# A graph block with gated experts on one core: the expert pairs all in the attention stage, and a combination in five parts with TensorE summing most pairs

## The reference

```
x = x + segment_sum(LN(x)[src] * edge_weight, dst) @ W + b       # layer 1
y = LN(x)
h = y @ W_gat                                   # 4 heads x 4 experts
a = leaky_relu(a_src[src] + a_dst[dst])         # 131072 edges + one loop per node
agg = segment_softmax(a) weighted sum of h[src], by dst, + b_gat
scores = LN(agg) averaged over the heads        # 4 per node
g = softmax over the 2 best scores, 0 for the other experts
out = x + sum over e of g[e] * (gelu(y @ W1[e] + b1[e]) @ W2[e] + b2[e])
```

## Time and profile before

| | us |
|---|---|
| median of 3 runs | 6031.14 (6027.12 to 6062.34) |
| the profiled execution, its own time | 6026.56 |
| its span (first to last instruction) | 6024.8 |

### The profile page before, as it was taken

One profiled execution on the slowest core, in us unless ns is written; L12 is line 12 of the kernel. 1 busy time (PEld: TensorE's weight loads), 2 busy tenths in 40 slices (PEclk: granted clock), 3 DMA queues, 4 the chain that ended last, 5 costly groups with the idle time before them and its releaser, 6 DMA issues. The chain is left out here.

```text
span 6024.8 us, 57614 instructions
## 1 busy us (share of the span) xinstructions
PE 3403.8 (56%) x13477; PEld 2557.7 (42%) x13478; DVE 1931.2 (32%) x4962; ACT 756.9 (13%) x2073; POOL 2722.3 (45%) x2817
## 2 busy tenths in 40 slices
PE   1354445455556776777822227964475665749266
PEld 0233333343444454555511116853354453628145
DVE  5435454645453444333300001221111020202359
ACT  4100000000000111111200001211011111202122
POOL 4465544454545555555377771043615243340420
PEclk6576666676767887888855558976677776869578
DMA  7422222222222333333100001111111111101348
GB/s 224 132 87 74 80 66 73 61 82 68 77 64 83 92 93 91 93 96 97 60 25 11 13 9 35 47 43 24 34 32 37 29 41 25 46 19 54 121 147 323
DMA packets 289866, 437.42 MB, mean 73 GB/s; under 512 B 60488, under 2 KB 223539, under 8 KB 288563
## 3 DMA queue, kind: packets, MB, share of 16 engines
q0 software_dynamic: 114208, 216.64, 13.5%
q1 hardware_dynamic: 77503, 127.56, 5.9%
q10 hardware_dynamic: 98004, 91.50, 4.7%
HBM read 329.96 MB, written 105.97 MB: 72 GB/s over the span
## 5 line engine op out<-in xcount | busy, mean ns | idle before, releaser
L633 POOL DMA_INDIRECT rows<-feats,src_t x1500 | 1457.2, 971 | 1285.3 <-PE node_sums L792 711.8
L1307 POOL DMA_INDIRECT got<-row_dram,src_sorted x1024 | 997.8, 974 | 1251.4 <-DMA state_dram<-got 914.8
L792 PE MATMUL node_sums<-rows,hot 128*128 x3904 | 1171.7, 459 | 667.9 <-issue 507.7
L792 PEld LDWEIGHTS node_sums<-rows,hot 128*128 128x128 f32 x3904 | 862.6, 230 | 945.7 <-issue 806.9
L1388 PE MATMUL d_hidden<-d_yt,w 128*128 128x256 f32 x2752 | 725.3, 402 | 584.4 <-issue 583.4
L1399 PE MATMUL d_expert<-w,hid 128*128 128x256 f32 x2752 | 723.2, 402 | 482.5 <-issue 480.6
L1388 PEld LDWEIGHTS d_hidden<-d_yt,w 128*128 128x128 f32 x2752 | 550.6, 201 | 727.7 <-issue 662.4
L1450 DVE TENSOR_TENSOR yo<-d_expert,b2r 128x512 f32<-128x512 f32 x172 | 119.0, 692 | 2230.8 <-remote 1391.9
L1399 PEld LDWEIGHTS d_expert<-w,hid 128*128 128x128 f32 x2752 | 552.1, 201 | 626.7 <-issue 560.1
L851 DVE TENSOR_SCALAR hot<-iota,rel,ew_t 128x128 f32<-128x128 f32 x1952 | 565.8, 362 | 99.2 <-issue 34.8
L1334 ACT ACTIVATE hid<-d_hidden,b1c 128x256 f32<-128x256 f32 x688 | 287.5, 471 | 2193.7 <-remote 1014.3
(11 more groups left out here) (310 smaller groups left out, 2450.2 us busy)
## 6 DMA issues: line engine op xcount, KB each, us to landing
ys<-y_dram SPq DMA_DIRECT2D x49, 1024.0 KB
y_dram<-yo ACTq DMA_DIRECT2D x172, 256.0 KB
rows<-feats,src_t POOLq DMA_INDIRECT x1500
got<-row_dram,src_sorted POOLq DMA_INDIRECT x1024
x_dram<-x ACTq DMA_DIRECT2D x98, 128.0 KB
xs<-x_dram SPq DMA_DIRECT2D x49, 256.0 KB
x_ring<-in_x ACTq DMA_DIRECT2D x97, 128.0 KB
state_dram<-got SPq DMA_DIRECT2D x8, 1536.0 KB, 5.1
```

Of the source, the lines that this page charges most:

```text
L633: pool.indirect_dma_start(rows[:, g % RING, j, :], None, feats, bass.IndirectOffsetOnAxis(ap=m.src_t[:, g * GT + j:g * GT + j + 1], axis=0 ...
L792: t = pe.matmul(psA[:, ds(((code >> 1) & 1) * 512, FEAT)], hot[:, r, j, :], rows[:, ds((code >> 2) & (RING - 1), 1), j, :], start=False, s ...
L1307: pool.indirect_dma_start(got[:, k, j, 0:ROWF], None, m.row_dram, bass.IndirectOffsetOnAxis(ap=m.src_sorted[:, b * BLOCK + j:b * BLOCK + j ...
```

## The change

1. The expert pairs all run in the attention block: `EARLY_PAIRS` is gone, 49 pairs stand there, and `late_experts` is removed. Block 6 of the edges gets pairs 45 and 46, and block 5 moves from pair 37 to 39; only block 7 is left for the time after the last pair.
2. SyncE loads the first four pairs for the combination (`AHEAD = 4`) right after it has stored block 0 of the states, in the attention block; the slots for it (`ys_ahead`, and part of `m.plan`) hold buffers of the earlier blocks before that. The clearing of `ns` moves to GpSimd's list in the attention block, ahead of the gathers.
3. The combination has 14 slots instead of 10 and five parts (22, 22, 22, 22, 10 tiles). SyncE asks for three more pairs, the three vectors, and seven more pairs at once, without waiting for the states.
4. Of the 49 pairs VectorE does 15 as before (every fourth of a part, every second in the last). The other 34 go to TensorE: ScalarE writes 8 diagonal matrices 128x128 per pair, each the gate of an expert (three pairs' worth in a ring), TensorE multiplies the expert outputs with them and x with the identity, 10 multiplications of 128x256 that add up in PSUM, and ScalarE copies the 128x512 sum back. ScalarE's answers for the gates of part n+1 now stand after 3, 5 and 7 of the TensorE pairs of part n.
5. Buffers of the first blocks are laid into memory that later serves the combination; the instructions on them are the same.

```
@@ constants
-EARLY_PAIRS = 43
-BLOCK_PAIR = [11, 15, 21, 27, 33, 37]
+BLOCK_PAIR = [11, 15, 21, 27, 33, 39, 45]
+SLOTS = 14
+AHEAD = 4
...
+def load_pair(eng, m, i, k, y, x):
+    eng.dma_start(y, m.y_dram...[:, 2 * i:2 * i + 2, :, :]).then_inc(m.s_load[k], 16)
+    eng.dma_start(x, m.x1_dram...[:, 2 * i:2 * i + 2, :]).then_inc(m.s_load[k], 16)
@@ attention_and_experts, sync
             for b in range(BLOCKS):
                 sp.wait_ge(s_fin, b + 1)
                 sp.dma_start(state_rows[...], got[...]).then_inc(s_kept[b % NBUF], 16)
+                if b == 0:
+                    for e in range(EXPERTS):
+                        sp.wait_ge(s_st[e], 16 * AHEAD)
+                    for k in range(AHEAD):
+                        load_pair(sp, m, k, k, m.ys_ahead[:, k], m.xs_ahead[:, k])
@@ attention_and_experts, gpsimd
             for t in range(SPREAD_BEFORE, TILES):
                 spread(pool, m, t)
+            pool.memset(m.ns, 0.0).then_inc(s_clear, 1)
@@ combine
-        PART = [0, 2 * SLOTS, 4 * SLOTS, T]
+        PART = [0, 22, 44, 66, 88, T]
+        BY_VECTOR = [i for n in range(PARTS) for i in range(PART[n] // 2, PART[n + 1] // 2)
+                     if (i - PART[n] // 2) % (4 if n < PARTS - 1 else 2) == 0]
+        BY_TENSOR = [i for i in range(PAIRS) if i not in BY_VECTOR]
+        SUMS, DIAGS = 4, 3
@@ combine, sync
+            for k in range(AHEAD, SLOTS // 2):
+                load_pair(sp, m, k, k, y_of(k), x_of(k))
             for n, a in enumerate((b_gat, gamma, beta)):
                 ...
+            for k in range(SLOTS // 2, SLOTS):
+                load_pair(sp, m, k, k, y_of(k), x_of(k))
+            for i in range(PAIRS):
+                store(i)
+                if 0 <= i - 2 < PAIRS - SLOTS:
+                    refill(i - 2 + SLOTS)
@@ combine, scalar
+            def diagonals(j):
+                if j >= DIAGS:
+                    act.wait_ge(s_mm, j - DIAGS + 1)
+                for t in range(2):
+                    for e in range(EXPERTS):
+                        q = act.activation(diag[:, j % DIAGS, t, e, :], m.ident[:], ACT.Identity,
+                                           scale=sc[:, tile + t, e:e + 1])
+                q.then_inc(s_dg, 1)
+            def out_of_psum(j):
+                act.wait_ge(s_mm, j + 1)
+                act.copy(x_of(BY_TENSOR[j]), psum[j % SUMS][:]).then_inc(s_done_t, 1)
...
+            for n in range(1, PARTS):
+                summed(n - 1, 0, 3)
+                weights(n)
+                summed(n - 1, 3, 5)
+                deviation(n)
+                summed(n - 1, 5, 7)
+                gate(n)
+                summed(n - 1, 7, PAIRS)
@@ combine, tensor
+            for j, i in enumerate(BY_TENSOR):
+                pe.wait_ge(s_in[i % SLOTS], loaded(i))
+                pe.wait_ge(s_dg, j + 1)
+                if j >= SUMS:
+                    pe.wait_ge(s_done_t, j - SUMS + 1)
+                for t in range(2):
+                    pe.matmul(psum[j % SUMS][:, t, :], m.ident[:], x_of(i)[:, t, :], start=True, stop=False)
+                    for e in range(EXPERTS):
+                        q = pe.matmul(psum[j % SUMS][:, t, :], diag[:, j % DIAGS, t, e, :], y_of(i)[:, t, e, :],
+                                      start=False, stop=(e == EXPERTS - 1))
+                q.then_inc(s_mm, 1)
```

397 lines of the change are left out of this document (124 added, 273 removed).

## The result

| | before | changed |
|---|---|---|
| median of 4 runs each, us | 6036.86 | 6096.56 (6083.2 to 6104.44) |
| the profiled execution's own time, us | 6026.56 | 6083.2 |
| its span, us | 6024.8 | 6080.1 |

The ratio of the changed kernel to the one before is 1.0087, with a 95% interval of 1.006 to 1.0114. It is slower by 0.9%, where the prediction said 6028 and practically no change, and its median lies above the predicted range (5980 to 6085).

What follows compares the result with a forecast made beforehand. Expert pairs on TensorE bound the attention block; the gathers' hold, then loads and work, the combination. 143.0 + 1 + 244 - 391.2 = -3.2 us on 6026.6, median 4.6 above: 6028; own range 6010 to 6045, wider 5980 to 6085.

Steps and rivals of the forecast that it cites:

- The attention block: Six more expert pairs add 168.4 us, one block of edges alone saves 25.4: +143.0 us, and +1 for the clearing.
- So the gates are ready at t = 49: Part 0's gates, counted from the combination's start: ready at 49 us instead of 160, a gain of 111 before other limits.
- A TensorE pair is 10 multiplications: In the combination: one pair takes 4.7 us at the low clock, 2.5 at the full one, 28 while held.
- my own rule: Beside gathers, some 70 to 90 multiplications pass, then one per 2.75 us; in the combination TensorE is free at t = 134.
- With pair 13 stored, loads are asked for up to pair 25: Combination's ring of 14 slots at t = 134: 23 pairs are left to load, 89.5 us.
- the 8 us of friction: Combination's end: loads finish at 236, work at 239, and 5 more for two close chains give t = 244.
- The price of a load: Combination: 3.89 us a pair, by the trace's 402 GB/s; by the 358 GB/s limit 4.39, some 11 us more.
- A: Rival, chance 0.20: in the combination TensorE is held from the start, 32 loads are left at 134, time 6060.
- D: Rival, chance 0.10: TensorE is never held in the combination, loads bind from t = 50, combination 203 us, time 5987.
- E: Rival, chance 0.08: combination loads run at the 338 GB/s seen beside gathers, 4.65 us a pair, +17.5 us, time 6045.
- C: Rival, chance 0.07: a combination pair's diagonals, multiplications and copy run serially, 7.9 us a pair, combination about 348, time 6132.
- of another kind than a count of multiplications: Stated failure condition: 134 of the combination's 244 us rest on the hold of TensorE being such a count.

Runs made afterwards that it cites:

- Experiment 1: The changed kernel with one gather of states per part in the combination instead of one per tile (93 of 98 left out): 6043.72 us, ratio 0.990.
- experiment 3: The changed kernel, where GpSimd waits in the combination after every 8 gathers until they have landed: median 6108.88 us, ratio 1.0003.
- experiment 2: The changed kernel, where VectorE sums pairs 0, 1 and 2 of part 0 instead of 0, 4 and 8: combination 296.8 us, 0.5 less.

## Why the prediction was wrong

**The attention block was right.** Six pairs at 28.06 us less one block alone: forecast +143 and +1 for the clearing, measured +144.1 from the first gather of rows to the prediction's t = 0 (141.2 and the 2.9 us of the old clearing). The pairs are 28.06 us apart still. The loads ahead cost nothing that can be seen; the clearing's 1.9 us fall ahead of the first gather of rows, where the prediction had put them into this stage at +1. The last expert output is out at 5741.8, and one block of edges stands behind it:

```profile
5741.08 0.69 DVE L1308 TENSOR_TENSOR yo<-d_expert,b2r 128x512 f32<-128x512 f32 x1 [2.76 <-PE d_expert L1257]
5741.69 0.22 DVE L1342 TENSOR_SCALAR limit<-seg_keep 128x128 f32<-128x128 f32 x1
```

**"So the gates are ready at t = 49"** failed, and it is the step that the miss starts from. They started at t = 33, 2 us later than forecast, and were ready at 81. I had priced them with the 17.2 us of the earlier trace rows, which were taken when no gathers ran. The held stretch of the kernel before had shown VectorE and ScalarE "with almost nothing to do", and I read that as no evidence of a hold on them; it was only no evidence. Experiment 1 has the same gates in 20.4 us, so it is the gathers that hold VectorE.

**"A TensorE pair is 10 multiplications"** was mis-sized by two. The rows count 20 records for the 10 of the program, and it was the records that the earlier trace rows count. (The 64 multiplications per layer in the account of the kernel before are records too; the program has 32 there. The price of an expert pair, 28.06 us, is a time and does not change by it.) With some 80 records ahead of the hold, 4 pairs would have passed by my own rule, not 8, and the next would take 55 us, not 28. Pair 6 would then be about the last stored by 134, and 30 loads, not 23, would be left: 7 x 3.89 = 27 us of the miss.

**"With pair 13 stored, loads are asked for up to pair 25"** failed with both. None was asked for in the hold: pairs 1 and 2 were summed by 5878, but ScalarE, held as well, copied them at 5898 and 5920, and SyncE asks for the first refill behind the store of pair 2. Against my 12 loads asked for by then this is 12 x 3.89 = 47 us, of which 27 are those above and, as what is left, 20 the hold on VectorE and ScalarE. This split follows my own rule and is not measured; experiments 1 and 3 show the hold as a whole. The remaining 6 to 7 us of the combination's 53 are small change: the refills start when I had them flow (139), but take 140 us to 6062 instead of 136, and the span ends 18 us behind them, where I had 15.5 with the 8 us of friction. VectorE waits for a load before it turns to the gates of part 4:

```profile
DVE xs L1721 <- DMA xs<-x_dram: 9.1, 1, 9.1
```

and ScalarE waits 7.5 us for these gates, so three TensorE pairs are left over when the loads end.

**The price of a load was right.** From 5930 to 6060 the DMA engines moved 403 GB/s, as in the earlier trace rows: 3.89 us a pair. The Trainium skill, page "DMA: Bandwidth & Descriptors", section Specifications, has about 358 GB/s as the limit from HBM for one core; the trace of the changed kernel lies above it over 130 us. It lies below the 425 GB/s that the same page of the Trainium skill, section Bandwidth, reports for a core that runs alone.

**The rivals.** A (held from the start, 6060) had the right sign and about half of the size, but not the mechanism: TensorE did its first 40 records at its pace. (Its 32 loads left go with loads asked for up to pair 16, not 17, a slip that leaves the sum as it is.) D (never held, 5987) is what experiment 1 makes of it by taking the gathers away: its 203 us for the combination against 201 measured. For E the premise shows again, 325 GB/s while the ring is filled beside gathers, but all refills came after the gathers and ran at full rate. C did not come: diagonals, multiplications and copies overlapped at 4.3 us a pair. In the prediction's last sentence the hold "of another kind than a count of multiplications" is named as what would break it. It is another kind: it falls on VectorE and ScalarE as on TensorE, and clearings of 2 us between the gathers undo it.

**What stays open** is what the engines are held by. The runs show when it comes and what lifts it, not which resource GpSimd's gathers take, nor whether the breaks count or the mean pace of the gathers. Each engine seems to get through some instructions of its own first (VectorE 26, ScalarE some 20, TensorE 73 to 86 records in the kernel before), and the runs do not tell whether that is a number or depends on the place in the program. In the changed kernel TensorE's 40 records end because it waits for diagonals, and after 22.6 idle us it does 14 more before it is held, so idle time seems to give back a part.

## What to carry to other kernels

Look for stretches where one engine works and all others show low shares with the releaser "issue": if it is GpSimd issuing indirect DMAs back to back, price every instruction beside it by held rows (here about 1.4 us each), on all engines, and test a pause of 2 us after every 8 before moving any work. Moving work out of such a stretch into one where its engine is the bound costs its full time (here 168 us), and what it was to free is freed only if the rest can run. Compare several stretches before calling a hold lifted: one of 100 us had 331 multiplications where its neighbours had 160 to 370. And count records of the trace against instructions of the program once for each kind, before a row of one is used as a price of the other.

## What the runs showed of the hardware

- After its first 20 to 45 us an unbroken run of gathers (128 rows each, one per 1.25 to 1.31 us) holds VectorE to one instruction per 1.40 us in the mean and delays a copy of ScalarE by up to 42 us. It holds TensorE to one record of a multiplication per 2.75 us; with its weight loads (36 and 37 records in 100 us) that is one instruction per 1.37 us, so the two engines are held to about the same pace. Held starts are mostly 1.4, 2.1 or 2.8 us apart.
- SyncE seems to be slowed as well: two issues stand 2.10 us apart beside gathers, two others shortly before 0.51 us (experiment 2). The transfers that had been asked for in the kernel before went on beside held engines (74 GB/s in the earlier trace rows).
- In the attention block, with a break after every 8 gathers, TensorE does 39 records in 100 us if the break is 1.07 us, 160 to 370 if it is 1.65 us, and 466 to 473, its full pace (clock 1.00), if it is 2.2 us. Breaks of 1.7 us after 16 win 36 of 2658 us, after 4 they win 899. The mean pace of the gathers falls along with it, from 78 to 59 in 100 us, and is not ruled out as the cause.
- It need not be a wait: GpSimd may be busy clearing a buffer in the break.
- At full pace TensorE (470 records per 100 us) and GpSimd (74 instructions, 78 us busy) work side by side.
